# Row maxima of causal attention: the mask added on DVE inside one fused add-and-reduce per head, instead of by mask products on PE

## The reference

```python
scores = jnp.einsum('bhqd,bhkd->bhqk', Q, K) / jnp.sqrt(jnp.float32(dk))
causal = jnp.tril(jnp.ones((Sq, Sk), dtype=bool))
scores = jnp.where(causal, scores, -jnp.inf)
attn = jax.nn.softmax(scores, axis=-1)
out = jnp.einsum('bhqk,bhkd->bhqd', attn, V)
```

## Time and profile before

| | |
|---|---|
| median of 3 runs | 502.17 us (502.12 to 503.55) |
| profiled execution, its own time | 502.17 us |
| its span, first to last instruction | 500.3 us |
| mean granted TensorE clock | 0.982 |
| PE / DVE / ACT / POOL busy | 458.4 / 308.2 / 210.1 / 193.1 us |

### The profile page before, as it was taken

How to read it: one execution, slowest core, us unless ns; L and a number is a source line. 1 busy time by engine, 2 the same in 40 slices (tenths; PEclk the granted TensorE clock), 3 DMA queues, 4 the chain that set the end, 5 groups by cost and what they waited for, 6 DMA issues and landing times.

```text
span 500.3 us, 10299 instructions
## 1 busy us (share of the span) xinstructions
PE 458.4 (92%) x3154; PEld 318.9 (64%) x3155; DVE 308.2 (62%) x651; ACT 210.1 (42%) x420; POOL 193.1 (39%) x204
## 2 busy tenths in 40 slices
PE   7868999999999999988699799999999999999993
PEld 6644344654447443554256366599999999999852
DVE  4984757477563757656674796855554554555436
ACT  2254666517572566517862352523322322322210
POOL 4123545114541336201512002126666766665420
PEclk9998999999999999999979899999999999999998
DMA  8593322422124121400298900014344344444279
GB/s 263 102 229 107 108 72 65 149 65 73 64 78 145 33 95 47 138 28 2 77 371 292 367 2 21 21 33 65 64 74 74 63 71 70 70 65 74 33 197 338
DMA packets 45574, 53.84 MB, mean 108 GB/s; under 512 B 7760, under 2 KB 41872, under 8 KB 44912
## 3 DMA queue, kind: packets, MB, share of 16 engines
q1 hardware_dynamic: 34320, 39.77, 24.8%
q0 software_dynamic: 7488, 10.31, 12.8%
q10 hardware_dynamic: 3744, 3.47, 2.7%
HBM read 27.09 MB, written 13.67 MB: 81 GB/s over the span
## 4 chain that ended last, share of the span: by engine, by line
PE 68%; DVE 10%; ACT 9%; DMA 6%; issue 5%; SPq 1%; DVEq 0%; ACTq 0%; POOLq 0%
PE set_a L624 7%; PE set_b L654 7%; PE set_a L924 6%; PE set_a L925 5%; PE set_a L923 5%; ACT attention L1074 5%; PE set_a L851 5%; PE set_a L675 4%; PE set_b L644 4%; DVE attention L1306 3%; PE set_b L861 3%; PE set_b L942 3%; PE set_a L832 3%; PE set_b L943 3%; PE set_b L944 3%
## 5 line engine op out<-in xcount | busy, mean ns | idle before, releaser
L1306 DVE TENSOR_REDUCE attention<-set_a 128x2 f32<-128x1024 f32 (+2 forms) x96 | 95.9, 1042 | 28.0 <-PE set_a L626 26.1
L1074 ACT ACTIVATE attention<-set_b 128x512 f32<-128x512 f32 (+1 forms) x176 | 88.4, 570 | 58.5 <-PE set_b L644 45.8
L528 POOL TENSOR_SCALAR_AFFINE_SELECT attention<-attention 128x512 f32<-128x512 f32 x64 | 40.8, 650 | 110.4 <-ACT attention L1074 110.4
L588 POOL DMA_INDIRECT sum_rows<-moe,token_of x39 | 61.8, 1585 | 43.9 <-issue 28.9
L644 PE MATMUL set_b<-attention 99*128 99x512 bf16 (+3 forms) x256 | 60.4, 310 | 13.6 <-ACT attention L1074 10.2
L624 PE MATMUL set_a<-attention 96*128 96x512 bf16 (+3 forms) x256 | 61.5, 306 | 5.6 <-DVE attention L1306 5.4
L580 POOL DMA_INDIRECT e_x<-normed_rows,token_of x39 | 39.4, 1010 | 63.7 <-DVE token_of L1504 37.3
L1173 ACT ACTIVATE moe<-set_a 128x384 f32<-128x384 f32 x39 | 19.1, 490 | 104.9 <-PE set_a L925 104.9
L1529 DVE TENSOR_TENSOR moe<-set_a,moe 128x384 f32<-128x384 f32 x39 | 21.8, 558 | 62.7 <-ACT moe L1173 62.7
L624 PEld LDWEIGHTS set_a<-attention 96*128 96x128 bf16 x256 | 25.3, 99 | 45.3 <-DVE attention L1306 18.0
L923 PE MATMUL set_a<-wup_hi,e_xT_hi 128*128 x156 | 53.1, 340 | 0.0
(11 more groups left out here) (167 smaller groups left out, 843.5 us busy)
## 6 DMA issues: line engine op xcount, KB each, us to landing
attention<-attention SPq DMA_DIRECT2D x182, 64.0 KB, 2.6
wup<-in_wupT SPq DMA_DIRECT2D x2, 3072.0 KB, 14.6
sum_rows<-attention SPq DMA_DIRECT2D x2, 2048.0 KB, 13.6
wup<-sum_rows SPq DMA_DIRECT2D x8, 512.0 KB, 7.0
attention<-in_ctxT SPq DMA_DIRECT2D x7, 512.0 KB, 6.2
w_down<-in_wdnT SPq DMA_DIRECT2D x3, 1024.0 KB, 5.0
x_res<-in_x SPq DMA_DIRECT2D x4, 512.0 KB, 7.1
out<-x_res ACTq DMA_DIRECT2D x8, 256.0 KB, 4.0
```

The lines of the kernel that those rows point to most:

```text
L588: g.indirect_dma_start(acc[i], bass.IndirectOffsetOnAxis(token_of[:, t:t + 1], 0), e_y[:, t % 2, :], None, compute_op=ALU.add).then_inc(ad ...
L1074: nc.scalar.activation(pT[k][:, h:h + heads, :], bank(par)[:, 0:heads * (S - k * P)], ACT.Exp).then_inc(b_free, 1)
L1306: v.tensor_reduce(dst, src, AX.X, ALU.max, negate=True).then_inc(a_free, 1)
```

## The change

The 256 mask products of the first pass go. The mask becomes a tile `mask_row` of 128 x 512 bf16, zero but for its last 128 columns, which are the old `maskb`; it lies in the attention region. `rowmax` no longer makes one reduction per job but one `tensor_tensor_reduce` per head: it reads the head's scores from PSUM and the last w columns of `mask_row`, adds them, multiplies by -1, writes the result back over the scores in PSUM, and puts the minimum over the row into that head's column of `mneg`. That is 16 instructions a group where there were 6. The wait for PE is carried by a semaphore increment of its own (`dve_turns`, which nobody waits for), ahead of the 2 or 4 instructions of a job; the last of them frees the job's half of set A.

```diff
--- before.py
+++ after.py
@@ -106,7 +106,6 @@
         gw = sb("gate_w", [P, C, 32])
         ident = sb("ident", [P, P])
         identb = sb("identb", [P, P], BF16)
-        maskb = sb("maskb", [P, P], BF16)
         beforeb = sb("beforeb", [P, P], BF16)
         onesb = sb("onesb", [P, P], BF16)
         expert_of = sb("expert_of", [P, NT], I32)
@@ -191,6 +190,8 @@
         bqc = part(2)
         bkc = part(2)
         zeros = part(D + WHO)
+        mask_row = part(S // 2).bitcast(BF16)
+        maskb = mask_row[:, S - P:S]
 
         xs = [attn, attnT.rearrange("p c (k d) -> p (c k) d", d=D)]
 
@@ -262,6 +263,7 @@
 
         a_full, a_free, b_full, b_free = sem("a_full"), sem("a_free"), sem("b_full"), sem("b_free")
         p_masked, rc_ready, pool_turns = sem("p_masked"), sem("rc_ready"), sem("pool_turns")
+        dve_turns = sem("dve_turns")
 
         lt_full, lt_read, lg_read, logits_full, route, d_ready, ex_ready, sel_ready = (sem(n) for n in
             ("lt_full", "lt_read", "lg_read", "logits_full", "route", "d_ready", "ex_ready", "sel_ready"))
@@ -466,7 +468,7 @@
             g.affine_select(out=ident[:], in_=ident[:], compare_op=ALU.not_equal, fill=1.0, base=0,
                             pattern=[[-1, P]], channel_multiplier=1).then_inc(consts, 1)
             g.memset(identb[:], 0.0).then_inc(pads, 1)
-            g.memset(maskb[:], 0.0).then_inc(pads, 1)
+            g.memset(mask_row, 0.0).then_inc(pads, 1)
             g.memset(beforeb[:], 0.0).then_inc(pads, 1)
             g.memset(onesb[:], 1.0).then_inc(pads, 1)
             g.memset(gw[:], 0.0).then_inc(pads, 1)
@@ -474,7 +476,7 @@
             g.affine_select(out=identb[:], in_=identb[:], compare_op=ALU.not_equal, fill=1.0, base=0,
                             pattern=[[-1, P]], channel_multiplier=1).then_inc(consts, 1)
 
-            g.affine_select(out=maskb[:], in_=maskb[:], compare_op=ALU.is_ge, fill=MASKED, base=0,
+            g.affine_select(out=maskb, in_=maskb, compare_op=ALU.is_ge, fill=MASKED, base=0,
                             pattern=[[-1, P]], channel_multiplier=1).then_inc(consts, 1)
 
             g.affine_select(out=beforeb[:], in_=beforeb[:], compare_op=ALU.is_ge, fill=1.0, base=0,
@@ -621,9 +623,8 @@
                 for i in range(heads):
                     h = g % 2 * HG + h0 + i
                     dst = pair(A, par)[:, i // in_bank, i % in_bank * w:(i % in_bank + 1) * w]
-                    mm(dst, qstack[0:ROWS, g // 2, h, k * P:w], kstack[0:ROWS, g // 2, h, 0:w],
-                       start=True, stop=False)
-                    last = mm(dst[:, k * P:w], identb[:], maskb[:], start=False, stop=True)
+                    last = mm(dst, qstack[0:ROWS, g // 2, h, k * P:w], kstack[0:ROWS, g // 2, h, 0:w],
+                              start=True, stop=True)
                 last.then_inc(a_full, 1)
 
             def maxima(n, par, g_count, first=False):
@@ -1295,15 +1296,16 @@
 
             def rowmax(j, n, par):
                 k, h, heads = R_JOBS[j]
+                w = (k + 1) * P
+                in_bank = heads // 2 if k else HG
                 dve.wait_ge(a_full, n + 1)
-                if k:
-                    src = pair(A, par)[:, :, 0:heads // 2 * (k + 1) * P].rearrange("p a (h n) -> p a h n",
-                                                                                 h=heads // 2)
-                    dst = mneg[:, k, h:h + heads].rearrange("p (a h) -> p a h", a=2)
-                else:
-                    src = pair(A, par)[:, 0, :].rearrange("p (h n) -> p h n", h=HG)
-                    dst = mneg[:, k, :]
-                v.tensor_reduce(dst, src, AX.X, ALU.max, negate=True).then_inc(a_free, 1)
+                dve.sem_inc(dve_turns)
+                for i in range(heads):
+                    src = pair(A, par)[:, i // in_bank, i % in_bank * w:(i % in_bank + 1) * w]
+                    last = v.tensor_tensor_reduce(out=src, in0=src, in1=mask_row[:, S - w:S], scale=-1.0,
+                                                  scalar=-LOWEST, op0=ALU.add, op1=ALU.min,
+                                                  accum_out=mneg[:, k, h + i:h + i + 1])
+                last.then_inc(a_free, 1)
 
             def max_parts(n, g_count):
 
```

## The result

| | before | after |
|---|---|---|
| median | 502.75 us (502.12 to 503.55, 4 runs) | 541.13 us (538.33 to 543.91, 4 runs) |
| profiled execution, its span | 502.17, 500.3 us | 538.72, 536.8 us |
| mean granted clock of PE | 0.982 | 0.937 |

The ratio is 1.0778, with an interval of 1.0737 to 1.082: 38 us slower, where 14 were forecast and 540 was the upper end of the range. The direction was right and the size was not. The four runs of the kernel after lie in two pairs, 538.3 and 538.7 us at a granted clock of 0.937, 543.6 and 543.9 at 0.925, so that a sum which meets their median to a microsecond does so in part by luck. The mean clock is the first sign that something else was at work than the lengths of DVE's instructions.

The account below looks back on a forecast made before the run. PE's list and DVE's first pass were taken to bound a slot almost at once. 6 x 1.04 + 6 x 0.97 + 1.38 + 0.1 + 0.1 + 0.2 = 13.8 us on 502.2 gave 516.0 us, range 501 to 540.

Parts of the forecast that it names:

- Mask products off PE: R 0 and R 1 of a plain slot ready 0.12 us earlier; the rest only makes PE wait longer.
- The handoff that was to eat this: Semaphore increment at R 0 and R 1 of a plain slot: 0.16 us against 0.04, eating the 0.12 gained.
- The fused instruction: DVE's first pass: 16 instructions take 7.82 us a group against 5.99, bounds 6.38 and 10.30.
- the two corrections: On each of DVE's 16 instructions: 0.09 us off for overlap, up to 0.155 on for the second output.
- the first rival: DVE's second output is an instruction of its own: 8.86 to 10.30 us a group, 532.6 to 555.7 us; chance 0.30.
- The walk through the slots: In the loop, 6 plain slots 1.04 us longer each, 6 with a projection 0.97 longer each.
- `max_parts` and the handoff take 0.95: Between the end of DVE's first pass and PE's MAX: 0.95 us, from 0.93 before and a little.
- so I cost no clock: PE's added idle time lowers no clock: a slot with PE busy 8.99 of 12.10 us stood at 1.00.
- the rivals: Second output its own instruction, 532.6 to 555.7 us (0.30); cost hidden, 502 (0.13); PE the bound, 491.9 (0.07).
- The signs I named: DVE busy up some 29 us to about 66%; plain-slot MAX about 9.0 us after DVE's first instruction, PE waiting there.
- the two signs that were to show the forecast wrong: MAX does not wait for DVE, or the fused instruction's pitch is far from the sum of the rows used.

Follow-up runs that it names:

- experiment 1: Kernel after with POOL's third split step (two subtractions) moved to DVE behind `max_parts`: 515.58 us against 501.50, ratio 1.0267.
- experiment 2: Kernel after with PE multiplying an unused tile ahead of MAX (44 products with a projection, 14 without): 523.02 us against 501.50, ratio 1.0416.
- experiment 8: Kernel after with POOL's third split step moved to DVE and 14 filling products ahead of each MAX of the loop: 511.95 us against 501.35, ratio 1.0217.
- Experiment 4: Kernel after with the 256 mask products put back on PE, so the mask is added twice: 541.70 us against 501.50, ratio 1.0788.
- Experiment 3: Kernel before without its 256 mask products, maxima taken over unmasked scores: 498.49 us against 501.50, ratio 0.993.
- its repetition: The kernel before without mask products and with unmasked maxima, run once more with more rounds: 497.33 us, ratio 0.9911.
- experiment 5: Kernel before with one of the six reductions of each group done twice, nothing of the change: 533.88 us against 501.35, ratio 1.065.
- experiment 6: Kernel before with POOL's third split step moved to DVE: 501.89 us against 501.35, ratio 1.0002.

## Why the prediction was wrong

**Where the 38 us are.** Experiments 1, 2 and 8 with the kernel after form a square: POOL's subtractions in the way or not, fillers or not.

| | no fillers | fillers |
|---|---|---|
| subtractions on POOL | 541.1 | 523.0 |
| subtractions moved | 515.6 | 512.0 |

The clock costs 541.1 - 523.0 = 18.1 us where the stall stands and 515.6 - 512.0 = 3.6 where it doesn't, the latter not clear of the scatter; the stall with the clock kept costs 523.0 - 512.0 = 11.1. The mean clocks agree for the first row: (1 - 0.937) x 536.8 = 33.8 us of full clock are missing in the kernel after and (1 - 0.968) x 521.4 = 16.7 in experiment 2, 17.1 apart, where these two profiled executions are 538.7 - 523.3 = 15.4 apart. For the row without the stall the same sum gives 8.5 (0.951 of 516.5 and 0.967 of 508.9), and the profiled executions are 518.5 - 510.9 = 7.6 apart.

The traces show where in the kernel it lies. From the first instruction of the first pass in the loop to that of the last batch (us):

| | from | to | length |
|---|---|---|---|
| before | 50.81 | 222.06 | 171.25 |
| experiment 8 | 53.28 | 230.34 | 177.06 |
| experiment 2 | 53.16 | 241.21 | 188.05 |
| after | 52.80 | 258.95 | 206.15 |

In the loop the longer pass and the select, net of the mask products, cost 5.8, POOL's subtractions 11.0 and the clock 18.1: 34.9 of the 36.5 us by which the span grew.

**Mask products off PE: open.** I counted 0.12 us a plain slot and nothing else. R 0 and R 1 hold two heads each, so by my own 0.06 four products stand ahead of the end of R 1, 0.24 us. The handoff that was to eat this took 0.19 in experiment 1 (63.78 to 63.97), near the 0.16 that I had. Experiment 4 found no difference clear of the scatter, but at another clock. Experiment 3 and its repetition show that they are worth 3 to 4.7 us, by themselves, while DVE keeps pace; that is more than I counted.

**The fused instruction: right in kind, a little too dear.** "7.82 us a group. I take that as the pitch" measured 7.14. Of the two corrections the overlap won: the second output exists, but its read runs inside the next instruction, and a 512-column head starts 0.64 us after the one before, against 0.60 for the plain additions of the earlier trace rows. So it adds some 0.04 to 0.60, where the first rival had 0.755. By the Trainium skill ("VectorE: DVE Perf Modes", section "Two Vector instructions with no wait between them") an operation that writes out its accumulator is two instructions, and the trace agrees: 256 rows of 141 ns beside 256. Its form was right in the rival, and its price, the 0.155 of an instruction that stands alone, was wrong. That 541 lies between the 532.6 and the 555.7 of this rival is luck: it needed 8.86 to 10.30 us a group.

**The walk through the slots: right up to MAX, too long behind it.** With 7.14 put into the prediction's steps, MAX of a plain slot comes at 119.72 + 7.14 - 1.26 + 0.95 = 126.55, 0.48 later than before, and S 10 of a projection slot ends at 108.52 + 7.14 + 0.95 + 1.15 = 117.76, 0.29 later. 6 x 0.48 + 6 x 0.29, some 0.7 for the group ahead of the loop and 0.3 for the rest give 5.6 us. From the end of the pass to MAX a plain slot now takes 144.39 - 143.03 = 1.36, as the select holds one instruction, where I put 0.95: 0.41 in each of the loop's 12 slots, 4.9. 502.2 + 5.6 + 4.9 = 512.7; experiment 8, which has neither the subtractions nor a slow clock in the loop, took 512.0. That is in part luck. MAX of a plain slot does come where the steps put it, 8.88 us after DVE's first instruction in experiment 1 (63.97 to 72.85) against 8.01 + 0.48 + 0.41 = 8.90. But in the loop the steps and the select make 4.6 + 4.9 = 9.5 us where the trace of experiment 8 shows 5.8, and ahead of the loop 2.5 came on (50.81 to 53.28) where I had 0.7. What makes good a part of the delay behind MAX stays open.

**The step that failed: "`max_parts` and the handoff take 0.95".** I took a duration from the trace of before and moved it later in time as if it were alone there. In the kernel after it took 1.36 in a plain slot and 131.07 - 127.89 = 3.18 in one with a projection. In the 6 projection slots of the kernel before POOL's subtractions (L514, 2.27 us for two) start 0.84 us after `max_parts` ended. The pass became longer by 7.28 - 5.98 = 1.30, the select held the second instruction, and the third came 0.09 us behind the start of POOL's subtraction (128.64, 128.73). So the last two instructions stood under the subtractions, and 2 x (1.085 - 0.18) = 1.8 us go on each of 6 slots: 10.9, against the 11.1 of the square. I had looked at what DVE delays on PE, and never at what runs on POOL in the microsecond into which DVE's work moved, though the rows for it were in the trace, and with them the first cast, held to 0.28. Experiments 1, 5 and 6 show it: the stall goes when POOL's subtractions go elsewhere, comes by lateness alone, and moving the subtractions gains nothing in the kernel before.

**The second that failed: "so I cost no clock".** I rested this on one slot of the last batch that stood at 1.00 with PE busy for 8.99 of 12.10 us. A sum over a slot doesn't show how the idle time lies in it. With 2.84 us of it in one piece ahead of MAX the clock was 0.50 afterwards; with 2.62 of these filled (experiment 2) it was 1.00. Two of the eight slow stretches stand behind plain slots, whose wait is 1.02, so a share of the term isn't the long wait's. This is the larger term, 18.1 us, and it wasn't among the rivals at all: all of mine were rates of DVE's instruction or bounds of PE's list. 502.2 + 5.6 + 4.9 + 10.9 = 523.6, against the 523.0 of experiment 2; the 18.1 are the measured rest to 541.1.

**The signs I named.** DVE's busy time rose by 36.4 us rather than 29, to 64% of the span rather than 66, and in part for another reason than mine: the passes went from 95.9 to 118.3 us, and `max_parts` from 12.9 to 26.8. PE does wait for the last step of `max_parts` in plain slots, as I said, but MAX came 144.39 - 133.67 = 10.7 us after DVE's first instruction there and not 9.0, as the first part of that slot ran at the lower clock. Neither of the two signs that were to show the forecast wrong came up: MAX waits for DVE, and the pitch is within a tenth of my sum. That net was too narrow.

## What to carry to other kernels

Before a step is moved later by a microsecond, look up what every other engine does in that microsecond, and above all whether DVE's new place lies beside two-input or select work of POOL: 0.18 us instructions became 1.09 here. A small instruction that is longer in some slots than in others, as the cast of 0.28 was, is worth a look before the change. Where a change lets PE wait in one piece, price the stretch behind the wait at the lower clock as a rival of its own; fillers in the wait tell in one run whether it is that. An engine with 62% of busy time can bind as hard as one with 92%: what counted was 0.36 us of room ahead of MAX, and 0.23 and 0.84 ahead of POOL's next instructions.

## What the runs showed of the hardware

DVE's instructions of 16 columns were held until POOL's instruction ended: a subtraction with two inputs in SBUF beside POOL's select (0.57 against 0.18) and beside POOL's subtraction (1.08), and a cast with one input beside POOL's select (0.28 in the kernel before) and beside POOL's subtraction (1.09 against 0.17). The fused instructions, with one input in PSUM and one in SBUF, kept their pitch of 0.64 to 0.65 while POOL's L511 ran from 120.88 to 123.15 in the projection slot shown above. The Trainium skill ("SBUF — State Buffer", section "Who interferes with whom") says that DVE and GpSimd share one pair of SBUF ports as an exclusive lock, that a DVE instruction with two SBUF inputs contends with a GpSimd instruction that reads SBUF, that in the modes which use both ports whichever issues first holds the pair for its whole instruction, and that a DVE instruction with at most one SBUF input, outside these modes, stays clear of it. The traces agree as far as they go: in the rows above POOL had started first and the held instructions ended with it, while the fused ones kept their pitch. That the cast runs in such a mode, and that the ports are what holds it, no run here shows.

It stays open what a `max_parts` without two inputs in SBUF would cost in the same place, and whether the handoff by a semaphore increment could be saved on the fused form; neither was tried.
